# Selective scan and expert routing on one core: the reciprocal of the routing denominator moved between the next unit's two scans, the third chunk's step size computed one and two units sooner, and the second chunk's row scatters moved to units 4 to 11 of the last chunk

## The chip, the cores and the metric

One core of one Trainium2 chip runs the whole program in one launch. The metric is the time of one execution on the device, in microseconds (us); lower is better. The engines are TensorE (PE, with its weight loads shown as PEld), VectorE (DVE), ScalarE (ACT), GpSimd (POOL) and SyncE (SP, which only issues transfers). Each engine runs its own instructions strictly in the order in which the program wrote them; semaphores order them between engines.

## What is computed

The input is x of shape (2, 1024, 128), which is 2048 tokens. Two sublayers follow, each with a residual and a layer norm. Cut to what matters here:

```python
x_in, z = split(x @ W_in); x_conv = silu(conv(x_in) + conv_b)        # 256 channels
Bm, Cm = split(x_conv @ W_x); dt = softplus(x_conv @ W_dt + b_dt)
h = exp(dt * A) * h + (dt * x_conv) * B_t                            # 16 states a channel
y = sum over the states of h * C_t, + x_conv * D, then * silu(z), @ W_out
x = layernorm(x + y)
logits = x @ w_g; the two best of 8 experts; probs = softmax over {top two, -1e9 elsewhere}
rank of each token in its expert (cumulative count), dropped at capacity 640
out = sum over the two experts of prob * (gelu(x @ c_fc[e]) @ c_proj[e])
x = layernorm(x + out)
```

## The kernel before, in words

**Chunks and units.** The tokens are worked on in four chunks of 512 (q = 0 to 3; "third chunk" is q = 2, "last chunk" q = 3), each chunk in 16 units, one for each state n of the scan. So there are 64 units, U = 16 q + n, and every engine has one loop `for U in range(LAST + 1)` over them. All times of the main loop below are told by unit. A unit consists of:

- ACT makes the decay exp(dt * A) of the unit (`decays`, L1074).
- PE spreads row n of B over the partitions (`spread_b`, L648) and DVE multiplies dt * u by it (`drives`, L1649), which gives the drive for two channel halves at once. `drive_beside(U)` says which unit's drive DVE makes between the two scans of unit U. For the 14 units in `TURNED` (4, 7, 10, 14, 19, 22, 26, 29, 43, 46, 51, 54, 57, 60) ACT and PE make the drive instead, so DVE has none beside that unit.
- DVE runs the recurrence as two scans of 512 steps, one for each half of the channels (`scan(U, 0)`, then `scan(U, 1)`, L1678).
- POOL multiplies both halves of the state by C (`multiply`, L1436). It waits for both scans.
- PE adds the product into the accumulator y in PSUM (`add_to_y`, L673 and L678).

Three states (`RING`) and four products (`PRODUCTS`) are kept: `scan(U, 0)` waits for the product of unit U - 3, and `multiply(U)` for the sum of unit U - 4.

**What stands between the units.** While the scan of chunk q runs, the output projection and the routing of chunk q - 1 are put between its units, at places written out by hand in tables indexed by q: `SORT`, `MARK`, `RANK`, `SCORE`, `EXPS`, `ADD`, `SHARE`, `PLACE`. The part that the change touches is the softmax weight of the two chosen experts, which goes back and forth between POOL and DVE:

- `score(q - 1)` on POOL at n = `SCORE[q]` (10, 11, 9 for q = 1, 2, 3), behind that unit's multiply: nine small operations. It ends with `above`, of which ACT takes the exponentials.
- `add_exps(q - 1)` on POOL one unit later (n = `ADD[q]`), behind that unit's multiply: three small operations that end with the denominator (L1497).
- `share(q - 1)` on DVE at n = `SHARE[q]` (12, 13, 11; units 28, 45 and 59): it waits for the denominator and takes its reciprocal (L1766, `share_ready`).
- `weigh(q - 1)` on POOL at n = `SHARE[q]`, behind that unit's multiply: it waits for `share_ready` and gives the two weights (L1501, `weight_ready`).
- `place_weights(q - 1)` on DVE at n = `PLACE[q]` = `SHARE[q]` + 1 (units 29, 46, 60, all of them in `TURNED`), after the unit's second scan: it waits for `weight_ready` and writes the weights into the rows to be sent (L1808).

**The scatters.** Each chunk has 8 indirect transfers (`scatter`, L1517) that POOL issues, four with the first choice and four with the second choice of 128 tokens each, into `slot_rows`. They stand behind a unit's multiply. Chunk 0's stand in units 29 to 36; chunk 1's in units 46, 47 and 48 to 53; chunk 2's in units 60 and 61 and then behind the loop, where the last chunk's 8 follow. A first-choice scatter of chunk q also waits until the second-choice scatters of the chunks before have landed.

**dt of the next chunk.** ACT computes softplus in steps (`take_dt_job`, `soften_exp`, `soften_log`), POOL adds its two parts (`finish_dt`, L1454) and multiplies by u (`times_u`, L1466), each of 128x1024 values, long before chunk q + 1 needs them. In chunk 1 these stand at n = 6 (`soften_log`, L1139), 7 (`finish_dt`) and 9 (`times_u`).

**The end of the loop.** The last unit's product is shared: POOL takes half 0, DVE half 1 (L1835). PE adds the products of units 62 and 63 (L673, L690), DVE gates the result (L1690), PE projects it, and sort, ranks and weights of the last chunk follow on DVE. Only then do the last chunk's scatters go out, and the experts can start when those have landed.

Of the kernel before, what the change touches and what calls it, by code (L numbers as in the profile page):

```python
# [21 lines left out]
NQ = TOKENS // CH  # L22
# [64 lines left out]
def layer_program(nc, x, W_in, channel_values, conv_rows, W_x, W_dt, A_log, W_out, w_g, c_fc, c_proj, out):  # L87
    with ExitStack() as ctx:
# [891 lines left out]
        def _(act):  # L980
# [252 lines left out]
            for U in range(LAST + 1):  # L1233
# [30 lines left out]
                if q < NQ - 1:  # L1264
                    first = 5 if q == 0 else q
                    if n == first:
                        take_bc(q + 1)
                    elif n == first + 1:
                        take_dt_job(q + 1, 0)
                    elif n == first + 2:  # L1270
                        take_dt_job(q + 1, 1)
                    elif n == first + 3:
                        soften_exp(q + 1)
                    elif n == (first + 4 if q == 0 else first + 5):
                        soften_log(q + 1)
# [99 lines left out]
        def _(gp):  # L1375
# [145 lines left out]
            def scatter_some(q, first, count):  # L1521
                for i in range(first, first + count):
                    scatter(i // TPC, TPC * q + i % TPC)

            EARLY = [D_STATE - n for n in PLACE]
            U_PLACE = (NQ - 1) * D_STATE + PLACE[NQ - 1]
            for U in range(LAST + 1):
                q, n = divmod(U, D_STATE)
                multiply(U)
                if q < NQ - 1:  # L1530
                    if n == (6 if q == 0 else q + 1):
                        split_bc(q + 1)
                    elif n == (10 if q == 0 else 6 + q):
                        finish_dt(q + 1)
                    elif n == (11 if q == 0 else 8 + q):
                        times_u(q + 1)
                if q:
# [6 lines left out]
                    if q == 1 and n == PLACE[q]:  # L1544
                        gp.wait_ge(rows_cleared, 16 * 2 * CLEARS)
                        gp.wait_ge(sent_tagged, 1)
                    if n >= PLACE[q] and U < LAST - 1:
                        scatter_some(q - 1, n - PLACE[q], 1)
                    if q >= 2 and n < RUNS // NQ - EARLY[q - 1]:
                        scatter_some(q - 2, n + EARLY[q - 1], 1)  # L1550
            scatter_some(NQ - 2, LAST - 1 - U_PLACE, RUNS // NQ - (LAST - 1 - U_PLACE))
# [27 lines left out]
        def _(dve):  # L1579
# [231 lines left out]
            for U in range(LAST + 1):  # L1811
                q, n = divmod(U, D_STATE)
                scan(U, 0)
                if drive_beside(U):
                    drives(drive_beside(U))
                scan(U, 1)
                if q:
# [6 lines left out]
                    if n == RANK[q] + 1:  # L1824
                        take_ranks(q - 1)
                        place(q - 1)
                    if n == SHARE[q]:
                        share(q - 1)
                    if n == PLACE[q]:
# [158 lines left out]
```

## Time and profile before

| | us |
|---|---|
| median of 3 runs | 385.12 (383.41 to 385.39) |
| the profiled execution, its own time | 384.32 |
| its span in the trace | 382.58 |
| busy: DVE / POOL / PE / ACT | 282.6 (74%) / 266.2 (70%) / 286.2 (75%) / 211.8 (55%) |
| units 0 to 63, from the first scan to the end of the last | 24.9 to 255.1 |
| expert layers and the last norm | 283 to 382.6 |

The profile is of one execution. Times in the rows are microseconds from the start of the span. In a timeline a row gives the start, the duration, the engine, the line of the kernel, the operation, the tile written <- the tiles read with their shapes, and how many instructions are merged into the row; in square brackets stands how long the engine was idle before it, and which instruction of another engine ended that wait ("issue" where the profile shows nothing that it waited for). Durations of neighbouring instructions overlap slightly, so the distance from one start to the next is what an instruction takes of its engine.

### The profile page before, as it was taken

What the parts mean: (1) busy time and instruction counts of PE and PEld (TensorE: products, weight loads), DVE (VectorE), ACT (ScalarE), POOL (GpSimd) and SP (SyncE); (2) the same over time, 40 slices, a digit from 0 to 9 for tenths busy, and PEclk for the clock granted to TensorE, in tenths of its full rate; (3) what the DMA queues carried; (4) which work ended last, traced back from release to release, by engine and by line L of the source; (5) the groups of instructions that cost most, each with busy time, mean ns of one, the idle gap of its engine ahead of it and who ended that gap; (6) DMA issues with size and microseconds to landing.
All of it is one profiled execution on the core that took longest, in us unless ns stands there. A gap on an engine that the chain in (4) does not pass through costs nothing. (4 is left out here: it accounts for less than half of the span.)

```text
span 382.6 us, 5173 instructions
## 1 busy us (share of the span) xinstructions
PE 286.2 (75%) x1566; PEld 207.6 (54%) x1566; DVE 282.6 (74%) x429; ACT 211.8 (55%) x425; POOL 266.2 (70%) x226
## 2 busy tenths in 40 slices
PE   8797889678866867786545899774289999998700
PEld 6445547456745544675433454332278888887600
DVE  2699889999999899999899889986021333334565
ACT  2858987969675684777737455744003323331305
POOL 4507689978888999999999876985710555556532
PEclk9999999999999868997885999899589999999965
DMA  7061079473354263232123211001152444222873
GB/s 233 6 224 55 2 240 286 135 194 127 89 168 137 82 199 117 69 100 82 55 73 122 74 64 55 3 15 42 43 155 79 118 126 125 82 82 76 240 204 110
DMA packets 35786, 42.90 MB, mean 112 GB/s; under 512 B 3862, under 2 KB 26331, under 8 KB 35760
## 3 DMA queue, kind: packets, MB, share of 16 engines
q1 hardware_dynamic: 32336, 37.38, 31.9%
q0 software_dynamic: 2304, 4.24, 3.4%
q10 hardware_dynamic: 1120, 0.97, 0.8%
q8 instruction: 12, 0.20, 0.2%
q14 instruction: 14, 0.11, 0.1%
HBM read 30.11 MB, written 12.79 MB: 112 GB/s over the span
## 5 line engine op out<-in xcount | busy, mean ns | idle before, releaser
L1436 POOL TENSOR_TENSOR product<-state,c_wide 128x1024 f32<-128x1024 f32 x64 | 149.9, 2347 | 37.1 <-DVE state L1678 27.5
L1074 ACT ACTIVATE psum<-dt,a_neg 128x512 f32<-128x512 f32 x96 | 65.0, 686 | 53.1 <-DVE state L1678 51.8
L678 PE MATMUL psum<-ident,product 128*128 128x128 f32 x384 | 56.1, 295 | 24.5 <-POOL product L1436 24.5
L678 PEld LDWEIGHTS psum<-ident,product 128*128 128x128 f32 x384 | 47.4, 152 | 35.0 <-POOL product L1436 32.1
L1678 DVE TENSOR_TENSOR_SCAN state<-psum,drive 128x512 f32<-128x512 f32 x52 | 62.0, 1212 | 2.5 <-ACT psum L1074 2.3
L1649 DVE TENSOR_TENSOR drive<-dtu,psum 128x1024 f32<-128x1024 f32 x50 | 60.0, 1199 | 4.6 <-PE psum L648 4.5
L1678 DVE TENSOR_TENSOR_SCAN state<-psum,carry,drive 128x512 f32<-128x512 f32 x48 | 60.0, 1269 | 0.2
L1563 POOL DMA_INDIRECT result_rows<-state,result_at x30 | 30.3, 1010 | 40.7 <-DVE state L1892 33.4
L1517 POOL DMA_INDIRECT slot_rows<-sent,scatter_at x32 | 32.9, 1028 | 10.7 <-issue 6.6
L912 PE MATMUL psum<-product,fc_sb 128*128 128x320 f32 x128 | 36.1, 435 | 1.1 <-DVE product L1860 1.1
L1857 DVE TENSOR_SCALAR tags<-c_wide 128x10 f32<-128x10 f32 x8 | 1.3, 164 | 43.4 <-PE psum L901 43.4
L1337 ACT ACTIVATE u<-psum 128x640 f32<-128x640 f32 x16 | 11.3, 704 | 38.6 <-PE psum L912 37.9
L673 PE MATMUL psum<-product,ident 128*128 128x512 f32 x60 | 29.4, 619 | 1.6 <-POOL product L1436 1.6
L912 PEld LDWEIGHTS psum<-product,fc_sb 128*128 128x128 f32 x128 | 22.8, 190 | 11.3 <-issue 2.7
L1337 ACT ACTIVATE z_tok<-psum 128x640 f32<-128x640 f32 x16 | 11.3, 704 | 27.6 <-PE psum L912 18.8
L664 PE MATMUL psum<-ident,drive_t 128*128 128x128 f32 x112 | 18.7, 296 | 8.6 <-DVE drive L1649 7.6
L723 PE MATMUL psum<-x_chan,w_conv 128*128 128x512 f32 x48 | 23.4, 614 | 1.6 <-ACT sent L1178 1.6
L1105 ACT ACTIVATE drive_t<-dtu_t,b_t 128x256 f32<-128x256 f32 x56 | 23.7, 494 | 1.0 <-PE psum L664 0.9
L664 PEld LDWEIGHTS psum<-ident,drive_t 128*128 128x128 f32 x112 | 14.4, 152 | 16.1 <-issue 14.3
L648 PE MATMUL psum<-bc_parts,selector 128*128 128x512 bf16 x50 | 20.0, 404 | 2.0 <-DVE state L1678 1.5
L1678 DVE TENSOR_TENSOR_SCAN state<-decay_sb,carry,psum 128x512 f32<-128x512 f32 x16 | 19.6, 1261 | 0.4 <-issue 0.4
L673 PEld LDWEIGHTS psum<-product,ident 128*128 128x128 f32 x60 | 11.5, 200 | 14.0 <-issue 10.7
(256 smaller groups left out, 527.1 us busy)
## 6 DMA issues: line engine op xcount, KB each, us to landing
c_wide<-c_rows SPq DMA_DIRECT2D x32, 512.0 KB
slot_rows<-blank SPq DMA_DIRECT2D x8, 325.0 KB, 4.6
c_wide<-slot_rows SPq DMA_DIRECT2D x8, 325.0 KB, 3.4
result_rows<-zeros SPq DMA_DIRECT2D x8, 256.0 KB, 5.1
late_rows<-zeros SPq DMA_DIRECT2D x8, 256.0 KB
fc_sb<-in_c_fc SPq DMA_DIRECT2D x8, 256.0 KB
proj_sb<-in_c_proj SPq DMA_DIRECT2D x8, 256.0 KB
c_wide<-result_rows SPq DMA_DIRECT2D x8, 256.0 KB, 5.5
```

What stands on the lines that cost most here:

```text
L664: last = nc.tensor.transpose(psum[:, turned_bank(U, d), j * P:(j + 1) * P], drive_t[:, j, d * P:(d + 1) * P], ident[:, :])
L673: nc.tensor.matmul(psum[:, Y_BANK + d, :], ident[:, :], product[:, i, d, :], start=False, stop=True, skip_group_check=True).then_inc(summe ...
L678: last = nc.tensor.matmul(y_part(j, d), product[:, i, d, j * P:(j + 1) * P], ident[:, :], is_transpose=True, start=False, stop=True, skip_ ...
L723: last = nc.tensor.matmul(psum[:, bank, :], w_conv[:, k, d * P:(d + 1) * P], x_of(q, k), start=(k == 0), stop=(k == D_CONV - 1))
L912: last = nc.tensor.matmul(psum[:, 2 + 2 * (h % 2) + s, 0:HALF], fc_sb[:, i, h * P:(h + 1) * P], rows_chan[:, i, s * HALF:(s + 1) * HALF], ...
L1074: nc.scalar.activation(psum[:, A_BANK + d, :], dt[:, q % 2, d, :], ACT.Exp, scale=a_neg[:, n:n + 1]).then_inc(decay_ready, 1)
L1105: nc.scalar.activation(drive_t[:, j, :], dtu_t[:, j, :], ACT.Copy, scale=b_t[:, q % 2, j, n:n + 1]).then_inc(drive_t_ready, 1)
L1436: nc.gpsimd.tensor_tensor(product[:, U % PRODUCTS, channels, :], state[:, U % RING, channels, :], wide, ALU.mult).then_inc(product_ready, 1)
L1517: gp.indirect_dma_start(out=slot_rows, out_offset=bass.IndirectOffsetOnAxis(ap=scatter_at[:, k, j:j + 1], axis=0), in_=sent[:, k, j, :], i ...
L1563: gp.indirect_dma_start(out=result_rows, out_offset=bass.IndirectOffsetOnAxis(ap=result_at[:, i, s:s + 1], axis=0), in_=rows_out[:, i, s, ...
L1649: nc.vector.tensor_tensor(drive[:, drive_number(U) % 2, :, :], dtu[:, q % 2, :, :], psum[:, b_bank(U), :].unsqueeze(1).to_broadcast([P, DT ...
L1678: nc.vector.tensor_tensor_scan(state[:, U % RING, d, :], decay, rows, before, ALU.mult, ALU.add).then_inc(scanned, 1)
```

## The change

Four edits:

- `share(q - 1)` on DVE moves from behind the second scan of unit `SHARE[q]` (28, 45, 59) to between the two scans of the unit after it (29, 46, 60), which are units without a drive on DVE.
- In chunk 1, `soften_log(2)` on ACT moves from n = 6 to n = 5.
- In chunk 1, `finish_dt(2)` on POOL moves from n = 7 to n = 6, and `times_u(2)` from n = 9 to n = 7. The other chunks' stay where they were.
- Chunk 1's 8 scatters move from units 46 to 53 to units 52 to 59 (n = 4 to 11 of the last chunk). Chunk 0's, chunk 2's and chunk 3's stay.

```diff
@@ ACT's loop
                     elif n == first + 3:
                         soften_exp(q + 1)
-                    elif n == (first + 4 if q == 0 else first + 5):
+                    elif n == first + (5 if q == 2 else 4):
                         soften_log(q + 1)
@@ POOL's loop
-            EARLY = [D_STATE - n for n in PLACE]
+            EARLY = D_STATE - PLACE[1]
...
-                    elif n == (10 if q == 0 else 6 + q):
+                    elif n == (10, 6, 8)[q]:
                         finish_dt(q + 1)
-                    elif n == (11 if q == 0 else 8 + q):
+                    elif n == (11, 7, 10)[q]:
                         times_u(q + 1)
...
-                    if n >= PLACE[q] and U < LAST - 1:
+                    if n >= PLACE[q] and q != 2 and U < LAST - 1:
                         scatter_some(q - 1, n - PLACE[q], 1)
-                    if q >= 2 and n < RUNS // NQ - EARLY[q - 1]:
-                        scatter_some(q - 2, n + EARLY[q - 1], 1)
+                    if q == 2 and n < RUNS // NQ - EARLY:
+                        scatter_some(0, n + EARLY, 1)
+
+                    if q == 3 and PLACE[q] - RUNS // NQ <= n < PLACE[q]:
+                        scatter_some(1, n - PLACE[q] + RUNS // NQ, 1)
@@ DVE's loop
                 scan(U, 0)
                 if drive_beside(U):
                     drives(drive_beside(U))
+                if q and n == SHARE[q] + 1:
+                    share(q - 1)
                 scan(U, 1)
...
-                    if n == SHARE[q]:
-                        share(q - 1)
                     if n == PLACE[q]:
                         place_weights(q - 1)
```

## Rows read from the trace of the kernel before

**Rows 1.** Last chunk: length; PE, PEld, DVE, ACT, POOL busy; PE's clock, DMA share, GB/s
```profile
196.90:255.10 58.20, 45.18 (x154) 24.15 (x152) 55.33 (x71) 36.42 (x72) 49.52 (x39) 0.85 0.17 57
```

**Rows 2.** Groups by line: the scatters and the logarithm of dt
```profile
L1517 POOL DMA_INDIRECT slot_rows<-sent,scatter_at x32 | 32.9, 1028 | 10.7 <-issue 6.6 <-DVE sent L1808 3.9 <-PE psum L678 0.2
...
L1139 ACT ACTIVATE soft<-soft 128x1024 f32<-128x1024 f32 x3 | 3.1, 1046 | 0.0
```

**Rows 3.** Timeline of DVE in chunk 1, units 27 to 29
```profile
118.88 1.26 DVE L1678 TENSOR_TENSOR_SCAN state<-psum,carry,drive 128x512 f32<-128x512 f32 x1
...
128.26 0.18 DVE L1766 RECIPROCAL denom<-denom 128x4 f32<-128x4 f32 x1 [1.23 <-POOL denom L1497]
...
130.81 0.14 DVE L1808 TENSOR_TENSOR sent<-weight,psum 128x8 f32<-128x8 f32 x1
```

**Rows 4.** Timeline of POOL in chunk 1, units 25 to 28 (times_u, then three multiplies)
```profile
117.93 2.35 POOL L1466 TENSOR_TENSOR dtu<-dt,u 128x1024 f32<-128x1024 f32 x1
120.25 2.34 POOL L1436 TENSOR_TENSOR product<-state,c_wide 128x1024 f32<-128x1024 f32 x1
...
125.14 2.36 POOL L1436 TENSOR_TENSOR product<-state,c_wide 128x1024 f32<-128x1024 f32 x1
...
128.18 2.36 POOL L1436 TENSOR_TENSOR product<-state,c_wide 128x1024 f32<-128x1024 f32 x1
```

**Rows 5.** Timeline of POOL in chunk 2, units 42 to 45
```profile
178.20 2.35 POOL L1436 TENSOR_TENSOR product<-state,c_wide 128x1024 f32<-128x1024 f32 x1 [0.93 <-issue]
...
190.61 0.20 POOL L1497 TENSOR_TENSOR denom<-denom,others 128x4 f32<-128x4 f32 x1
190.76 2.35 POOL L1436 TENSOR_TENSOR product<-state,c_wide 128x1024 f32<-128x1024 f32 x1
193.07 0.21 POOL L1501 TENSOR_TENSOR weight<-exps,denom 128x8 f32<-128x8 f32 x1
```

**Rows 6.** Timeline of DVE in chunk 2, units 45 and 46
```profile
190.84 0.18 DVE L1766 RECIPROCAL denom<-denom 128x4 f32<-128x4 f32 x1 [1.58 <-POOL denom L1497]
...
193.31 0.17 DVE L1808 TENSOR_TENSOR sent<-weight,psum 128x8 f32<-128x8 f32 x1
```

**Rows 7.** Timeline of POOL in the last chunk, the multiplies of units 55 to 62
```profile
226.47 2.37 POOL L1436 TENSOR_TENSOR product<-state,c_wide 128x1024 f32<-128x1024 f32 x1 [1.20 <-PE psum L673]
231.16 2.37 POOL L1436 TENSOR_TENSOR product<-state,c_wide 128x1024 f32<-128x1024 f32 x1 [2.32 <-DVE state L1678]
234.64 2.36 POOL L1436 TENSOR_TENSOR product<-state,c_wide 128x1024 f32<-128x1024 f32 x1 [1.11 <-issue]
...
239.54 2.35 POOL L1436 TENSOR_TENSOR product<-state,c_wide 128x1024 f32<-128x1024 f32 x1
...
242.72 2.35 POOL L1436 TENSOR_TENSOR product<-state,c_wide 128x1024 f32<-128x1024 f32 x1
...
245.41 2.36 POOL L1436 TENSOR_TENSOR product<-state,c_wide 128x1024 f32<-128x1024 f32 x1 [0.19 <-issue]
...
249.37 2.34 POOL L1436 TENSOR_TENSOR product<-state,c_wide 128x1024 f32<-128x1024 f32 x1 [0.36 <-issue]
...
252.93 3.57 POOL L1436 TENSOR_TENSOR product<-state,c_wide 128x1024 f32<-128x1024 f32 x2
```

**Rows 8.** Timeline of DVE: unit 60's weights, and behind the last scan
```profile
245.26 0.17 DVE L1808 TENSOR_TENSOR sent<-weight,psum 128x8 f32<-128x8 f32 x1
...
255.15 1.91 DVE L1835 TENSOR_TENSOR product<-state,c_wide 128x512 f32<-128x512 f32 x1
259.05 0.69 DVE L1690 TENSOR_TENSOR z_last<-z_last,psum 128x512 f32<-128x512 f32 x1 [1.99 <-PE psum L690]
```

**Rows 9.** Timeline of PE: the sum of unit 62
```profile
256.21 1.88 PE L673 MATMUL psum<-product,ident 128*128 128x512 f32 x4
```

**Rows 10.** Busy time by stretch, columns as in Rows 1, where PE's clock falls
```profile
120.00:122.00 2.00, 0.00 (x0) 0.00 (x0) 2.00 (x3) 0.69 (x1) 2.00 (x2) 1.00 0.81 236
...
124.00:126.00 2.00, 2.00 (x8) 1.30 (x7) 2.00 (x3) 1.59 (x6) 1.67 (x6) 0.50 0.01 4
```
## The prediction

> **What bounds the kernel now.** I read the busy time by stretch first, then the timelines of DVE and POOL side by side around each place that the diff touches, then PE's behind the last scan. The stretch of the last chunk shows DVE busy 55.3 us of 58.2, POOL 49.5 and PE 45.2 [rows 1]: DVE is the engine that carries the loop, and the time of the loop is DVE's work plus DVE's waits. Two of those waits are the ones that the change goes for. In chunk 1 DVE stands 1.23 us before its reciprocal [rows 3], in chunk 2 1.58 us [rows 6], both times until POOL's last operation on the denominator. In the last chunk no wait is shown there. But POOL comes close behind: a multiply takes 2.32 us from start to start (193.07 - 190.76 is 2.31, 120.25 - 117.93 for `times_u` 2.32) [rows 4, 5], a unit 58.2 / 16 = 3.6, and everything else that POOL does has to fit between. A scatter is 1.03 us of POOL by itself [rows 2]; from one multiply to the next with a scatter between they are 252.93 - 249.37 = 3.56 us apart [rows 7], so a scatter costs POOL 3.56 - 2.32 = 1.24 us. Idle time of POOL is what pays for moved scatters, and the question of each part is whether POOL is early or late where it lands.
>
> **Part 1, chunk 1: dt sooner and the reciprocal.** Today `times_u` sits between the multiplies of units 25 and 26 [rows 4], so unit 26's starts at 120.25, though its scans end where the next scan starts plus the small overlap, about 118.95 [rows 3]. With `times_u` and `finish_dt` moved two and one units up, POOL is free at 117.93 and takes unit 26 right behind its scans, at about 119.07. The rest is POOL's own sequence: from unit 26 to 27 4.89 us with the score between, from 27 to 28 3.04 with the sum of the exponentials [rows 4]. So unit 27 starts at 123.96 and unit 28 could at 127.00. The denominator is ready now at 128.26, 3.12 us after unit 27's start; it will be at about 127.08. DVE came to the reciprocal at 128.26 - 1.23 = 127.03. So this move alone takes nearly all of the wait away; the move of the reciprocal behind scan(29, 0) gives another 1.2 us of room. What is late next is the weights. POOL multiplies unit 28 from about 127.16 on, `weigh` ends 2.52 us later (193.28 - 190.76) at 129.68 [rows 5]. DVE needs 0.18 + 2.37 us for reciprocal and two scans (130.81 - 128.26 - 0.18) and is at `place_weights` at 129.58, so it waits some 0.1 us and writes at about 129.71 where it wrote at 130.81 [rows 3]: 1.1 us gained. The cost: the two moved operations of 2.36 us meet POOL in units 22 and 23, where they put product 23 and 24 about 1.2 us later; POOL has caught up by unit 25, and the ring allows two units. On ACT the logarithm of 1.05 us [rows 2] now runs before the two copies of y in unit 21, not after; PE takes them and then spreads B for a drive. Bounds for that are 0 and 1.05; I take 0.1, near the lower end, because the delay has to pass through PE, which works ahead of DVE, before it meets DVE. Part 1 comes to -1.0 us, with bounds -1.23 (the whole wait) and -0.1.
>
> **Part 2, chunk 2: the reciprocal.** Nothing ahead of it on POOL is moved here. DVE is at the reciprocal 1.58 us before 190.84, at 189.26; two scans take 193.31 - 190.84 - 0.18 = 2.29 us [rows 6]. After the change it makes scan(46, 0) first, until 190.40, and waits 0.44 for the denominator, which still ends at 190.81 [rows 5]. Then reciprocal and scan(46, 1), until about 192.17, and there stands `place_weights`, which waits for `weigh`. `weigh` is behind the multiply of unit 45, which starts at 190.76 in any case, and ends at 193.28; `place_weights` starts at 193.31 today. So it will start at 193.31 again: of the 1.58 us, 0.44 stay at the reciprocal and 1.14 turn up before the weights. POOL is what is late, since unit 42's multiply at 178.20, the last before which it was idle, with `times_u`, score, the sum and `weigh` between. Part 2 is worth 0; bounds -1.14 (if the weights did not hold DVE) and 0.
>
> **Part 3: the scatters.** They leave units 46 to 51, where no scan or drive of DVE's waited for a product, so nothing is gained there. Two of the eight stay in units 52 and 53. Six are new in units 54 to 59, 7.4 us of POOL's time. Idle time of POOL that can take them [rows 7]: 1.20 before unit 55, 2.32 before 56, 1.11 before 57. So the scatters of units 54 and 55 cost nothing, and the one of 56 delays unit 57 by 0.1. From there POOL has no room. Unit 58's multiply goes from 239.54 to 234.72 + 4.90 + 1.24 = 240.86 (4.90 is the distance in the rows, the score between). Unit 59's: 240.86 + 3.04 + 1.24 = 245.14, where it is 242.72 now (3.04 as in chunk 1, where no wait lies between). `weigh` ends 2.52 us behind at 247.66. DVE comes to `place_weights` of unit 60 at about 245.2 and today does it at 245.26 [rows 8]; it will wait until 247.68. That is +2.4 us on DVE, and a wait in the place of the one that the change removes. The denominator itself, ready at 240.86 + 3.12 = 243.98, meets DVE between the scans at about 243.7, and its 0.3 are part of those. Then unit 60's multiply starts at 247.6 + 1.24 = 248.85 (now 245.41), and with 3.56 us each unit 61's at 252.4 (249.37) and unit 62's at 256.0 (252.93), 3.1 us later. The last scan ends 2.4 us later less about 0.2 of small waits that are then covered, at 257.3, where 255.15 is the start of what follows it now [rows 8].
>
> The end: PE adds the product of unit 62 at 256.21 now [rows 9], 1.0 us after it was ready at 252.93 + 2.32 = 255.25: PE comes to it behind work that waits for the last scan. It will be ready at 258.3, and PE free for it at 258.4, so the sum comes 2.2 us later; DVE's half product, gating, sort and the last scatters follow at the same distances. New too: the second-choice scatter in unit 59 stands ahead of the first-choice one in unit 60 that waits for its landing, with a multiply of 2.3 us between. I take that as enough; if it is not, a wait of up to one more such length would come on top. The six scatters behind the loop end before the last weights are there, with 3.9 us to spare now (POOL's wait for L1808) [rows 2], and 3.9 - 3.1 + 2.2 = 3.0 then. Part 3 comes to +2.2; bounds 0 and +3.1, and +5.4 with a slow landing.
>
> DVE's half product behind the last scan takes 1.91 us where an operation of the same shape takes 0.69 [rows 8]; it starts beside POOL's multiply. The Trainium skill (SBUF — State Buffer, "Who interferes with whom") has a DVE instruction with two SBUF inputs contend with a GpSimd one that reads SBUF, and the later one wait fully; the row agrees. By that rule the half product could wait for POOL's later end, near 260 at worst, about when PE would come to it anyway, so the sum would stay.
>
> **The sum.** -1.0 + 0 + 2.2 = +1.2 us. The profiled execution took 384.32 (span 382.58) and would take 385.5. The median of the runs is 385.12, 0.8 above it; I give the forecast on the median: 386.3, which is 0.3% up. About 0.5%, 1.9 us, is what a measurement of this kernel can tell from no change.
>
> **Rivals.** *POOL has the room.* If the scatters did not delay the weights of unit 60 (because POOL's idle time of 1.20 + 2.32 + 1.11 + 0.19 = 4.8 us in units 55 to 60 [rows 7] was usable as a whole, or units 46 to 51 gave some back) and DVE gained in chunk 2, the sum would be -1.0 - 1.14 = -2.1 us: 383.0. For it speaks that both waits are plain in the rows; against it that `weigh` ended 0.03 us before DVE used it in chunk 2 and that the last POOL idle time before unit 58 is 1.11 us. It decides by whether unit 59's multiply starts before 243. Chance 0.09. *Parts cancel or none does anything*, with the wait at the weights of unit 60 near 1 us: 384 to 385.5. Chance 0.2.
>
> *The clock of PE at the end (slower).* PE's granted clock fell to 0.5 (1.2 GHz) in chunk 1 behind a stretch without work: none in the one from 120, half clock in the one from 124 [rows 10]. In the last chunk it averages 0.85 [rows 1]. With products 59 to 62 up to 3.1 us later, PE does the same work behind unit 58 in a longer time. A sum takes it 1.88 us [rows 9], and a product comes every 3.56. If that drops the clock, the matmuls behind the last scan, of which unit 62's sum is 1.88 us and unit 63's the same again with the projection as much once more, run at half speed for half or all of 5.6 us: +2.8 to +5.6, 3 in the middle of what is likely, so 386.3 + 3 = 389.3. It decides by the granted clock behind 255; the gaps that I count, 3.56 - 1.88 = 1.7 us, are shorter than the empty stretch in chunk 1. Chance 0.14, with the slow landing in it. The Trainium skill (TensorE: Matmul & The Clock Gate, "Why this matters for your kernels") has the clock go down when PE is idle between bursts. By that rule the rows agree.
>
> **The numbers.** Forecast 0.57, the rivals 0.09, 0.2 and 0.14. The range takes the first rival in and goes up to the clock's: 383.0 to 389.3. Slower by over 0.5% (above 387.05): the clock's 0.14, and a fifth of the forecast's case, where part 3 costs its upper bound: 0.26 together. Faster by over 0.5% (below 383.2): 0.09. Within: 0.65.
>
> **What would show it.** Right: no wait before the reciprocal of unit 29; a wait of about 0.4 before the one of unit 46 and one of about 1.1 before its weights; about 2.3 us of DVE's waiting before the weights of unit 60, ended by POOL's L1501; unit 59's multiply above 2 us behind its scan; units 52 to 62 on POOL without idle time from 57 on. Wrong: a unit 60 without a wait, or a chunk 2 that is shorter by 1 us, or PE's half clock behind 255.

## The result and the profile after

The changed kernel takes 389.53 us (median of 6 runs, 387.6 to 390.42), the kernel before 385.19 in the same runs (383.41 to 385.44): ratio 1.0121, 95% interval 1.0094 to 1.0148. It is 1.2% slower. The forecast was 386.3, 0.3% slower; the result lies 0.2 us outside its range. The profiled execution took 390.21 us, its span is 388.5.

The medians lie 4.3 us (1.1%) apart, the two profiled executions 5.9: the one of the kernel before is 0.9 us under its median, the one of the changed kernel 0.7 above. The stretches below are those of these two executions. The starts of the scans divide the 5.9 us. "Chunk 1" runs from the first scan of unit 16 to that of unit 32, "chunk 2" to that of unit 48, "last chunk" to the end of the last scan.

| us | to unit 16 | chunk 1 | chunk 2 | last chunk | behind it |
|---|---|---|---|---|---|
| before | 79.51 | 58.38 | 58.97 | 58.19 | 127.5 |
| after | 79.80 | 59.42 | 60.23 | 61.75 | 127.3 |
| forecast | | -1.0 | 0 | +2.2 | 0 |
| measured | +0.3 | +1.0 | +1.3 | +3.6 | -0.2 |

The last chunk has DVE's work unchanged (55.29 us, 55.33 in [rows 1]) in a stretch that is 3.6 us longer, and so has POOL (49.38 and 49.52). The added time is waiting. (The forecast has 2.4 us of waiting in the last chunk, less 0.2 that it covers, and an end that moves with it.) The busy time of that stretch, columns as in [rows 1]:

```profile
199.44:261.19 61.75, 44.93 (x154) 23.37 (x152) 55.29 (x71) 36.42 (x72) 49.38 (x39) 0.89 0.16 54
```

The timeline of DVE answers to [rows 3], [rows 6] and [rows 8]: reciprocal and weights of each chunk (L1769 and L1811 are L1766 and L1808 of before), then what follows the last scan.

```profile
128.83 0.15 DVE L1769 RECIPROCAL denom<-denom 128x4 f32<-128x4 f32 x1
130.29 1.28 DVE L1681 TENSOR_TENSOR_SCAN state<-decay_sb,carry,psum 128x512 f32<-128x512 f32 x1 [1.31 <-issue]
131.49 0.14 DVE L1811 TENSOR_TENSOR sent<-weight,psum 128x8 f32<-128x8 f32 x1
...
133.21 1.22 DVE L1652 TENSOR_TENSOR drive<-dtu,psum 128x1024 f32<-128x1024 f32 x1 [0.39 <-PE psum L648]
...
193.42 0.18 DVE L1769 RECIPROCAL denom<-denom 128x4 f32<-128x4 f32 x1 [0.45 <-POOL denom L1497]
...
195.88 0.17 DVE L1811 TENSOR_TENSOR sent<-weight,psum 128x8 f32<-128x8 f32 x1 [1.07 <-POOL weight L1501]
...
247.43 0.18 DVE L1769 RECIPROCAL denom<-denom 128x4 f32<-128x4 f32 x1 [0.43 <-POOL denom L1497]
...
251.60 0.17 DVE L1811 TENSOR_TENSOR sent<-weight,psum 128x8 f32<-128x8 f32 x1 [2.70 <-POOL weight L1501]
...
261.28 2.86 DVE L1838 TENSOR_TENSOR product<-state,c_wide 128x512 f32<-128x512 f32 x1
265.43 0.69 DVE L1693 TENSOR_TENSOR z_last<-z_last,psum 128x512 f32<-128x512 f32 x1 [1.29 <-PE psum L690]
```

No wait is left before the reciprocal of unit 29. The 1.58 us of unit 46 have become 0.45 and 1.07. Unit 60 waits 0.43 + 2.70 us, both times for POOL. Not in the forecast: 1.31 us between the two scans of unit 29.

The timeline of POOL, answering to [rows 7]: the multiplies of units 57 to 60 and the scatters between them.

```profile
237.96 2.37 POOL L1436 TENSOR_TENSOR product<-state,c_wide 128x1024 f32<-128x1024 f32 x1
...
243.21 1.09 POOL L1517 DMA_INDIRECT slot_rows<-sent,scatter_at  x1 [0.32 <-issue]
244.33 2.36 POOL L1436 TENSOR_TENSOR product<-state,c_wide 128x1024 f32<-128x1024 f32 x1
...
247.20 0.20 POOL L1497 TENSOR_TENSOR denom<-denom,others 128x4 f32<-128x4 f32 x1
247.99 1.04 POOL L1517 DMA_INDIRECT slot_rows<-sent,scatter_at  x1 [0.59 <-PE psum L673]
249.06 2.35 POOL L1436 TENSOR_TENSOR product<-state,c_wide 128x1024 f32<-128x1024 f32 x1
251.36 0.20 POOL L1501 TENSOR_TENSOR weight<-exps,denom 128x8 f32<-128x8 f32 x1
251.73 1.03 POOL L1517 DMA_INDIRECT slot_rows<-sent,scatter_at  x1 [0.16 <-issue]
252.78 2.37 POOL L1436 TENSOR_TENSOR product<-state,c_wide 128x1024 f32<-128x1024 f32 x1
```

And PE ahead of unit 29, first before, then after. Before, the sum of a product (L678) waited 3.14 us for POOL, and the convolution (L723) followed with no idle time ahead of it:

```profile
122.64 1.58 PE L678 MATMUL psum<-ident,product 128*128 128x128 f32 x8 [3.14 <-POOL product L1436]
...
124.87 2.77 PE L723 MATMUL psum<-x_chan,w_conv 128*128 128x512 f32 x4
127.48 0.60 PE L664 MATMUL psum<-ident,drive_t 128*128 128x128 f32 x4
```
```profile
122.19 1.09 PE L678 MATMUL psum<-ident,product 128*128 128x128 f32 x8 [1.98 <-POOL product L1436]
...
125.56 3.78 PE L723 MATMUL psum<-x_chan,w_conv 128*128 128x512 f32 x4 [1.83 <-ACT u L1143]
129.14 1.06 PE L664 MATMUL psum<-ident,drive_t 128*128 128x128 f32 x4
```

The turned drive that the second scan of unit 29 reads (L664, 129.14) stands behind a convolution that starts 0.7 us later and runs at half clock. DVE's "<-issue" wait ends 130.29, when that drive is there. In both kernels the convolution starts right behind ACT's copy of its first half out of the bank (L1143), first before, then after:

```profile
124.14 0.67 ACT L1143 ACTIVATE u<-psum,channel_sb 128x512 f32<-128x512 f32 x1
```
```profile
124.84 0.67 ACT L1143 ACTIVATE u<-psum,channel_sb 128x512 f32<-128x512 f32 x1
```

### The profile page after: what moved, and what is told of

It reads as the page before. It is cut to its first block and busy times, and to the rows that moved or that the text cites. A ratio compares the mean times of both kernels' runs of the same rounds, so it can differ in the third digit from the quotient of the medians.

```text
span 388.5 us, 5173 instructions
## 1 busy us (share of the span) xinstructions
PE 288.8 (74%) x1566; PEld 207.3 (53%) x1566; DVE 284.1 (73%) x429; ACT 211.8 (55%) x425; POOL 265.8 (68%) x226
## 5 line engine op out<-in xcount | busy, mean ns | idle before, releaser
L678 PE MATMUL psum<-ident,product 128*128 128x128 f32 x384 | 55.6, 293 | 22.4 <-POOL product L1436 22.2
L1652 DVE TENSOR_TENSOR drive<-dtu,psum 128x1024 f32<-128x1024 f32 x50 | 60.1, 1202 | 6.4 <-PE psum L648 6.4
L678 PEld LDWEIGHTS psum<-ident,product 128*128 128x128 f32 x384 | 47.1, 151 | 32.7 <-POOL product L1436 29.3
L673 PE MATMUL psum<-product,ident 128*128 128x512 f32 x60 | 28.5, 603 | 6.4 <-POOL product L1436 6.4
L723 PE MATMUL psum<-x_chan,w_conv 128*128 128x512 f32 x48 | 24.4, 637 | 2.7 <-ACT u L1143 1.8
L664 PE MATMUL psum<-ident,drive_t 128*128 128x128 f32 x112 | 19.2, 302 | 7.2 <-DVE drive L1652 6.2
L664 PEld LDWEIGHTS psum<-ident,drive_t 128*128 128x128 f32 x112 | 14.8, 156 | 15.5 <-issue 13.7
```

What stands on the lines that cost most here:

```text
L664: last = nc.tensor.transpose(psum[:, turned_bank(U, d), j * P:(j + 1) * P], drive_t[:, j, d * P:(d + 1) * P], ident[:, :])
L673: nc.tensor.matmul(psum[:, Y_BANK + d, :], ident[:, :], product[:, i, d, :], start=False, stop=True, skip_group_check=True).then_inc(summe ...
L678: last = nc.tensor.matmul(y_part(j, d), product[:, i, d, j * P:(j + 1) * P], ident[:, :], is_transpose=True, start=False, stop=True, skip_ ...
L723: last = nc.tensor.matmul(psum[:, bank, :], w_conv[:, k, d * P:(d + 1) * P], x_of(q, k), start=(k == 0), stop=(k == D_CONV - 1))
L1652: nc.vector.tensor_tensor(drive[:, drive_number(U) % 2, :, :], dtu[:, q % 2, :, :], psum[:, b_bank(U), :].unsqueeze(1).to_broadcast([P, DT ...
```

## The experiments

All ratios are to the kernel before, run beside it on the same chip.

**Each part alone.** e1 moves only the reciprocal:

```diff
                 scan(U, 0)
                 ...
+                if q and n == SHARE[q] + 1:
+                    share(q - 1)
                 scan(U, 1)
...
-                    if n == SHARE[q]:
-                        share(q - 1)
```

> Before with only the reciprocal moved between the next unit's scans. Theory 1 (POOL is late; the reciprocal is not what DVE needs): each wait turns up again at the weights one scan later. Chunk 1: the reciprocal of unit 29 waits under 0.1 us, the weights wait until about 130.7, as before, gain 0.1 us; chunk 2: 0.44 us at the reciprocal and 1.1 at the weights of unit 46, gain 0; chunk 3: nothing. Sum 385.1 within 0.5. Theory 2 (the move itself costs, since a reciprocal between two scans breaks them up): the whole difference of the changed kernel, some 2 us or more, is here already: 387 or above. Theory 3 (the move frees DVE as it reads): 382.4.

Measured: 385.98 us, 1.0009 (0.999 to 1.0028), as the first theory has it. The profile shows waits moved from the reciprocals to the weights, 1.23 to 1.00 and 1.58 to 0.45 + 1.06:

```profile
127.80 0.18 DVE L1766 RECIPROCAL denom<-denom 128x4 f32<-128x4 f32 x1
127.98 1.28 DVE L1678 TENSOR_TENSOR_SCAN state<-decay_sb,carry,psum 128x512 f32<-128x512 f32 x1
130.26 0.17 DVE L1808 TENSOR_TENSOR sent<-weight,psum 128x8 f32<-128x8 f32 x1 [1.00 <-POOL weight L1501]
```

e2 has only `soften_log`, `finish_dt` and `times_u` sooner:

```diff
-                    elif n == (first + 4 if q == 0 else first + 5):
+                    elif n == first + (5 if q == 2 else 4):
...
-                    elif n == (10 if q == 0 else 6 + q):
+                    elif n == (10, 6, 8)[q]:
...
-                    elif n == (11 if q == 0 else 8 + q):
+                    elif n == (11, 7, 10)[q]:
```

> Before with only the third chunk's dt sooner. Theory 1: POOL has the denominator of chunk 1 ready at about 127.1, so the 1.23 us wait in unit 28 goes, but PE makes the first half of the fourth chunk's convolution at its half clock and turns unit 29's second drive only behind it: DVE waits 1.0 to 1.3 us before the second scan of unit 29, and 0.3 before the drive of unit 23 (the copies of y behind the logarithm). Sum +0.3 to +1.5 us, 385.5 to 386.7. Theory 2 (this part is clean, as forecast): 384.0 to 384.3, no wait in unit 29.

Measured: 385.85 us, 1.0009 (0.9991 to 1.0027). The 1.23 us are gone, but units 23, 29 and 30 wait 0.30 + 0.96 + 0.22 and chunk 1 is 59.21 us, 0.8 longer; chunk 2 is 60.14, 1.2 longer, with 1.5 us of waits in units 40 and 41. The profile of e2 has both extra lengths of the changed kernel. It is of an execution 1.3 us above e2's median; by the medians this part costs 0.09% (-0.09 to +0.27%).

e3 has only the scatters (the last hunks of POOL's loop):

> Before with only the second chunk's scatters in units 52 to 59. Theory 1: POOL is full from unit 56 on; unit 59's multiply starts 3 us or more behind its scan, the denominator is about 2 us late for the reciprocal behind unit 59's scans and the weights of unit 60 wait another 1 to 1.5. Units 59 to 61 take 3.2 to 3.6 us more, the run 388.4 to 389.0. Theory 2 (the clock of PE at the tail and in chunk 3 is what costs): unit 60 as before, chunk 3 long by its units 48 to 54 and by the sums behind the last scan.

Measured: 387.94 us, 1.0079 (1.0053 to 1.0105). Chunk 1 is as before (58.40), chunk 2 0.4 us longer (59.34), the last is 60.89, 2.7 longer:

```profile
244.18 0.18 DVE L1769 RECIPROCAL denom<-denom 128x4 f32<-128x4 f32 x1 [1.62 <-POOL denom L1497]
...
248.35 0.17 DVE L1811 TENSOR_TENSOR sent<-weight,psum 128x8 f32<-128x8 f32 x1 [1.54 <-POOL weight L1501]
```

The wait at unit 60 is POOL's and the scatters' alone. e4 is the changed kernel without them (e1's and e2's edits):

> The changed kernel with the scatters where they were before. Theory 1: no wait at the weights of unit 60; what is left is the convolution at half clock in units 29 and 30: 385.5 to 387. If the three parts just add up, this is e1 + e2 - before, and the changed kernel is this + e3 - before. Theory 2 (parts fight): above 388 although the scatters are back.

Measured: 386.07 us, 1.0017 (0.9997 to 1.0036); chunks 59.26, 60.14 and 58.62, unit 60 waits 0.27. 0.17% here (0.7 us) and 0.79% in e3 (3.0 us) are 0.96% of the 1.21%; the rest is within the intervals. The profile of e4, too, is of an execution above its median, by 1.3 us.

**The same scatters two units sooner**, on e4 (`q == 3 and 2 <= n < 10`, units 50 to 57):

> The changed kernel with the second chunk's scatters in units 50 to 57, two units sooner. Theory 1 (POOL's idle time ends at unit 57): only the scatter of unit 57 is too many. It puts unit 58's multiply 1.2 to 1.5 us later and unit 59's 1.3 us behind its scan; the weights of unit 60 wait 1.0 to 1.5 us where the changed kernel's wait 2.7 and e4's 0.3. The run is 1 us above e4's, 387. Theory 2 (the scatters cost by themselves, wherever they stand in the last chunk): as the changed kernel, 389.5. Theory 3 (any place before the weights is free): as e4, 386.1.

Measured: unit 60 waits 0.48 + 1.00 us. The last chunk is 59.92, 1.3 longer than in e4: in the profile the first theory's wait is there. The median, 388.39 us (1.0098, 1.0071 to 1.0126), is 2.3 above e4 and not the 1 expected; the profiled span is only 0.9 above, since e4's profiled execution is 1.3 us above e4's median and e5's is at its own. By its median e5 lies between the first theory (387) and the second (389.5) and can't be told from the changed kernel (1.0094 to 1.0148).

**What holds chunk 1.** In e6, on e4, one of the two taps of the convolution in unit 28 goes to unit 29 (1 + 3 in the place of 2 + 2):

```diff
-                        conv_job(3, 1, range(2 * (n - 12), 2 * (n - 11)))
+                        conv_job(3, 1, range(n - 12, (1, D_CONV)[n - 12]))
```

> e4 (reciprocal and dt as in the change, scatters as before) with the convolution of the fourth chunk's second half split 1 + 3 taps over units 28 and 29 in place of 2 + 2, so that less of it stands ahead of unit 29's second turned drive. Theory 1a (it is only the order on PE): the 1.3 us wait before the second scan of unit 29 is gone, and the run is 1.3 us below e4's. Theory 1b (PE is the bound of units 28 to 30 as long as its clock is at half): the wait moves to unit 30's drive, which stands behind the same matmuls; units 28 to 32 together are as long as in e4, 14.9 us, the run 386.1.

Measured: 385.68 us, 1.0018 (0.9995 to 1.004). Unit 29's wait is gone and the drive of unit 30 waits in its place; PE as a whole is late:

```profile
130.24 0.17 DVE L1808 TENSOR_TENSOR sent<-weight,psum 128x8 f32<-128x8 f32 x1 [0.28 <-POOL weight L1501]
130.41 1.28 DVE L1678 TENSOR_TENSOR_SCAN state<-psum,carry,drive 128x512 f32<-128x512 f32 x1
132.95 1.22 DVE L1649 TENSOR_TENSOR drive<-dtu,psum 128x1024 f32<-128x1024 f32 x1 [1.25 <-PE psum L648]
```

So e8, on e4, gives PE work to do in its idle time: the spread of B for unit 30 is done 9 times, the first turned drive of unit 29 5 times, into the same place.

```diff
+                for _ in range(8 if U == 30 else 0):
+                    nc.tensor.matmul(psum[:, b_bank(U), :], selector[:, n, :], bc_parts[:, q * CH:(q + 1) * CH], start=True, stop=True)
...
+                for _ in range(5 if U == 29 and d == 0 else 1):
```

> e4 with repeated matmuls on PE (unit 30's B row 9 times, unit 29's first turned drive 5 times, both with the same result) where PE stood idle ahead of the fourth chunk's convolution. Theory 1 (the granted clock is the cause in chunk 1): the clock stays at 1.0 from 118 to 130, a half of the convolution takes 1.9 us and not 3.8, the wait before unit 29's second scan falls from 1.3 to at most 0.4 and unit 30's goes; the run is 1 to 1.7 us below e4's, 384.4 to 385.1, unless a later stretch loses the clock in its place. Theory 2 (order, or ACT's copy alone): the wait stays above 1 us, 386.1.

Measured: 385.03 us, 0.9997 (0.9975 to 1.0018), 1.0 us under e4 by the medians, with intervals that overlap. In the profiles the work added to PE took 1.5 us out of chunk 1 (57.78 us, 59.26 in e4). The busy time by stretch, of the changed kernel and then of e8 (PE's clock is the third number from the end):

```profile
120.00:130.00 10.00, 6.19 (x22) 3.56 (x22) 8.87 (x13) 6.12 (x12) 8.96 (x15) 0.68 0.63 168
```
```profile
120.00:130.00 10.00, 10.00 (x59) 6.81 (x58) 9.60 (x16) 6.21 (x13) 9.00 (x17) 1.00 0.57 189
```

e5 shows the same without any added work. Up to unit 49 it is the changed kernel, but in its profiled execution the half clock came at 112.0 to 118.9, and from 120 to 130 the granted clock was 1.00. The same convolution then takes 1.99 us behind an even longer wait for ACT, and unit 29 has no wait before its second scan:

```profile
126.25 1.99 PE L723 MATMUL psum<-x_chan,w_conv 128*128 128x512 f32 x4 [2.47 <-ACT u L1143]
128.07 0.60 PE L664 MATMUL psum<-ident,drive_t 128*128 128x128 f32 x4
```

Unit 27, which is near the earlier half clock, waits 1.04 us for PE instead.

**The weights sooner, in the place of the change.** e7 is the kernel before with the sum of the exponentials right behind the score, and `weigh` ahead of the multiply:

```diff
+                if q and n == SHARE[q]:
+                    weigh(q - 1)
                 multiply(U)
...
                         score(q - 1)
-                    if n == ADD[q]:
-                        add_exps(q - 1)
-                    if n == SHARE[q]:
-                        weigh(q - 1)
+                        add_exps(q - 1)
```

> The kernel before, with the small operations on POOL taken ahead of the multiplies that they stood behind: the sum of the exponentials right behind the score, weigh ahead of unit SHARE's multiply. Reciprocal, dt and scatters as before. Theory 1 (what DVE waits for in chunks 1 and 2 is a multiply that POOL makes first): both waits, 1.23 and 1.58 us, go and none turns up at the weights; the last scan ends 2 to 2.8 us sooner, the run is 382.5 to 383.5. Theory 2 (POOL's total work is the bound, the order does not matter): the waits turn up elsewhere, at the ring or the drives; 385.2.

Measured: 384.3 us, 0.9979 (0.9955 to 1.0003), above the 382.5 to 383.5 of the first theory and no gain that is clear of noise. Both waits of [rows 3] and [rows 6] are gone, but PE is late next: unit 30 waits 1.02 us, unit 47 1.80.

```profile
189.03 0.15 DVE L1765 RECIPROCAL denom<-denom 128x4 f32<-128x4 f32 x1
...
191.32 0.14 DVE L1807 TENSOR_TENSOR sent<-weight,psum 128x8 f32<-128x8 f32 x1
...
194.42 1.22 DVE L1648 TENSOR_TENSOR drive<-dtu,psum 128x1024 f32<-128x1024 f32 x1 [1.80 <-PE psum L648]
```

**Keeping PE busy everywhere: a miss first.** e9 (on e8), e10 (on e7, with e8's repeats) and e11 (on the changed kernel, with them) put transposes of the identity into the bank of PE's next job, ahead of the sum of a product (20 in unit 38, 12 in unit 39; e10 and e11 also in units 45 to 50).

> The kernel with parts 1 and 2 and with PE kept busy ahead of chunk 1's end, and now also repeated transposes of the identity on PE in its idle stretches of units 38 (20 of them) and 39 (12); their results are overwritten. Theory (PE's low clock makes the waits of units 40 and 41): the granted clock stays at 1.0 from 158 to 172, DVE's 0.64 in unit 40 and 0.65 + 0.24 in unit 41 shrink to 0.5 in sum or less, the loop is 1.0 shorter, about 384.0 us. Rival (the order of PE's work alone makes them late, whatever the clock): the three waits stay at about 1.5 in sum and the time at 385.0.

> The version that I expect to be the fastest: the kernel before with the weights sooner (sum of the exponentials right behind the score, weights ahead of the multiply), and with PE kept busy by repeated work in its idle stretches (spread of B 9 times for unit 30, the turned drive of unit 29 5 times, transposes of the identity in units 38, 39, 45, 46, 48 and 50). Theory (with both reciprocal waits gone what is left is PE at half clock): the waits of 1.02 in unit 30, 0.74 in units 39 and 40, 1.80 in unit 47 and 1.00 in unit 52 lose 2.5 of their 4.6 us, about 382 us, under both kernels. Rival (the waits come from POOL's products or from the order on PE): 384.3 as with the weights sooner alone.

> The changed kernel itself, with PE kept busy by the same repeated work. Theory (the 1.2 us by which chunk 1 and the 1.2 us by which chunk 2 are longer than before come from PE's clock, and the scatters hold DVE 3.4 us at unit 60 whatever the clock): 1.31 in unit 29, 0.39 in unit 30 and 1.6 in units 40 and 41 shrink to 1.0 in sum; the 0.43 + 2.70 of unit 60 stay; about 387.2 us against 389.5, which leaves about +2 to the kernel before. Rival (the clock is no part of it): 389.5.

Measured: 387.05 (1.0065, 1.0045 to 1.0085), 391.93 (1.0193, 1.0167 to 1.0218) and 395.14 us (1.0293, 1.0261 to 1.0325). The added work waits for the bank, which ACT empties late, and all of PE's queue behind it waits too, the spread of B for the drive of unit 40 with it (e9, timelines of PE, then of DVE):

```profile
160.58 3.43 PE L709 MATMUL psum<-ident 128*128 128x128 f32 x20 [2.92 <-ACT y_chan L1181]
163.81 1.72 PE L681 MATMUL psum<-ident,product 128*128 128x128 f32 x8
```
```profile
165.78 1.22 DVE L1661 TENSOR_TENSOR drive<-dtu,psum 128x1024 f32<-128x1024 f32 x1 [3.05 <-remote]
```

In e10 and e11 DVE waits another 5.12 and 6.25 us in unit 46. On the clock in chunk 2 these runs decide nothing. In chunk 1 e9 and e11 repeat e8, e11 on the changed kernel itself (57.78 and 57.79 us; 59.42 without the repeats). And they say that what fills an idle stretch must not wait for anything itself.

**With work that is ready.** e12 (on e4), e13 (on e7), e14 (on the changed kernel) and e15 (on the kernel before) all have the same edit: repeats of spreads and turned drives whose bank and inputs are free.

```diff
+            SPREADS = {30: 9, 50: 10}
+            TURNS = {(29, 0): 5, (43, 0): 5, (46, 0): 3, (46, 1): 4, (51, 0): 5, (51, 1): 3}
+            AHEAD = {32: 10, 38: 12, 39: 6}
...
+                if U in AHEAD:
+                    spread_b(drive_beside(U + 1), AHEAD[U])
                 if q and n < 2:
                     add_to_y(U - 2)
```

> Parts 1 and 2 with PE kept busy in chunk 1 as in the run before, and by repeated work that is ready in its idle stretches of chunk 2 and 3: the next spread of B 10, 12 and 6 times ahead of the sum of a product in units 32, 38 and 39, the spread of unit 50 10 times, and turned drives 3 to 5 times in units 43, 46 and 51. Theory (clock): the granted clock stays at 1.0 from 134 to 172 and from 200 to 213, the waits of units 40 and 41 (1.53 in sum) fall to 0.9 or less (0.76 + 0.24 was what the delayed run kept at full clock), the 1.79 of unit 52 to 1.0 or less, about 383.7 us against 385.0. Rival (order of the work): both waits stay, 385.0.

> The kernel before with the weights sooner, and the same repeated work. Theory (clock): 4.6 us of waits in units 30, 39, 40, 47 and 52 fall to 2.5 or less, about 382.5 us, under the kernel before by 0.6%. Rival: the wait of 1.80 in unit 47 is for PE's order (a turned drive and a spread behind a product that POOL finishes late) and stays, 384.

> The changed kernel with the same repeated work. Theory (1.03 + 1.25 us of chunks 1 and 2 and 0.7 at unit 52 are the clock, 3.4 at unit 60 are POOL's): about 387.0 us, the waits of unit 60 unchanged at 0.43 + 2.70. Rival (the clock has no part beyond chunk 1): 388.3.

> The kernel before with the same repeated work on PE as e12. Theory (parts 1 and 2 are worth the forecast 1 us where PE's clock is held): 384.5 us, 1.0 above e12, with the waits of 1.23 and 1.58 before the reciprocals in units 29 and 46 still there and those of units 40, 41 and 52 small. Rival (the waits of parts 1 and 2 are replaced by others with the clock held too): 383.5, as e12.

| | us (median) | ratio, 95% interval | chunk 1 | chunk 2 | last chunk | behind it |
|---|---|---|---|---|---|---|
| e15: before | 384.01 | 0.9973 (0.995 to 0.9997) | 58.41 | 58.81 | 56.90 | 128.1 |
| e12: parts 1 and 2 | 383.46 | 0.9954 (0.9932 to 0.9976) | 57.80 | 58.82 | 56.92 | 127.7 |
| e14: the changed kernel | 387.24 | 1.0047 (1.0018 to 1.0077) | 57.80 | 59.00 | 59.86 | 130.0 |
| e13: weights sooner | 383.06 | 0.995 (0.9926 to 0.9973) | 58.21 | 57.14 | 56.24 | 130.1 |

In the changed kernel the repeated work takes 2.3 us off (387.24 against 389.53): 4.7 in the loop of the profiled executions, of which 2.7 are lost again behind it. Of the waits over 0.4 us that e15 does not have, POOL's are left, those of unit 46 (0.42 + 1.07, in the place of e15's 1.58) and those of unit 60 (e14):

```profile
242.24 0.18 DVE L1778 RECIPROCAL denom<-denom 128x4 f32<-128x4 f32 x1 [0.49 <-POOL denom L1506]
...
246.40 0.17 DVE L1820 TENSOR_TENSOR sent<-weight,psum 128x8 f32<-128x8 f32 x1 [2.71 <-POOL weight L1510]
```

Busy time by stretch for units 38 to 41 and 48 to 51, columns as in [rows 1], first the changed kernel, then e14:

```profile
160.00:172.00 12.00, 7.35 (x39) 6.40 (x38) 10.88 (x10) 8.12 (x15) 11.41 (x7) 0.72 0.20 62
198.00:213.00 15.00, 8.11 (x36) 6.12 (x36) 15.00 (x14) 9.61 (x20) 9.59 (x5) 0.61 0.24 84
```
```profile
160.00:172.00 12.00, 11.76 (x88) 9.23 (x85) 12.00 (x12) 9.94 (x22) 11.72 (x7) 1.00 0.26 93
198.00:213.00 15.00, 10.55 (x61) 7.22 (x61) 15.00 (x14) 8.55 (x17) 10.16 (x5) 1.00 0.23 71
```

DVE has no wait in units 40, 41 and 52 of e14, where it had 0.62, 1.00 and 1.83 us. For these units the rival of order is out: the same sequence at full clock is in time. In unit 30 of e7 and e13 it is not the clock: the wait is 1.02 and 1.01 us, with the clock at 1.00 from 126 to 132 in both, and the spread of B stands behind a sum that waits for POOL's product (0.63 and 0.56 us) and a half of the convolution.

**Behind the loop.** In e13 and e14 the stretch behind the last scan took 130 us, in the other kernels so far 126.6 to 129.1. In e13 PE ends its 26 matmuls of the identity 1.23 us before the rows are there, and the first expert's layer takes 6.23 us; e12 has 4.54. First e13, then e12:

```profile
280.00 0.77 PE L910 MATMUL psum<-ident,c_wide 128*128 128x128 f32 x5 [1.23 <-DMA c_wide<-slot_rows]
281.85 6.23 PE L921 MATMUL psum<-product,fc_sb 128*128 128x320 f32 x16 [1.08 <-DVE product L1868]
```
```profile
282.04 0.71 PE L910 MATMUL psum<-ident,c_wide 128*128 128x128 f32 x5
283.83 4.54 PE L921 MATMUL psum<-product,fc_sb 128*128 128x320 f32 x16 [1.08 <-DVE product L1869]
```

e16 is e13 with `range(34)` for `range(26)` there:

> e13 with 34 in the place of 26 matmuls of the identity on PE (about 2 us more at half clock, 1.2 at full) ahead of the turning of the first rows. Theory (in e13 this work ended 1.2 us before the rows were there, PE's granted clock fell at 281.9, and the first expert's layer took 6.23 us where it takes 4.54): no half clock behind 280, the stretch from the last scan to the end 127.5 and not 130.0 us, 381 us in the median. Rival (the 2.5 us come from the loading of the rows or of the weights): 130.0 us, 383 us.

Measured: 383.06 us, 0.9942 (0.992 to 0.9964), the median of e13. The layer is back at 4.54 us, which gives 1.7, but the first rows are turned 29.9 us behind the last scan (29.1 in e13, 28.3 in e12), and the stretch is 130.3 us. The longer fill took 0.7 us of it. Another 1.2 us were lost behind the start of the last expert's layer (31.6 us from there to the end, 30.4 in e13 and 30.5 in e12), by what is not shown. The theory was right on the cause of the slow layer and wrong on the gain.

## Why the prediction was wrong, step by step

In short: the sum's +1.2 us left out that TensorE's clock could fall where DVE follows PE closely inside the loop, took the earlier logarithm as nearly free, and priced the scatters 0.7 us too low. By the ratios the scatters alone cost 3.0 us (e3; forecast +2.2), parts 1 and 2 together 0.7 (e4, -0.1 to +1.4; forecast -1.0), and the whole change 4.7 (3.6 to 5.7; forecast +1.2).

**Part 2 was right.** 0.44 and 1.14 us were forecast, 0.45 and 1.07 came; e12 and e15 have 58.82 and 58.81 us for chunk 2. The reciprocal and the weights hang on one queue of POOL's, and moving DVE's reader moves only the wait.

**Part 1 was right on POOL and wrong on ACT and PE.** The step that failed is the cost of the earlier logarithm: "because the delay has to pass through PE, which works ahead of DVE", taken as 0.1 out of 0 to 1.05. With the clock held the part gives 57.80 - 58.41 = -0.6 (e12 and e15): the wait of 1.27 us before the reciprocal goes and 0.28 come back before the weights, which is the forecast's -1.0, but the drive of unit 23 waits 0.30 us for PE, behind copies of y that ACT makes 1.2 us later in the chunk (102.08, before 100.64). At the clock that the kernel has, chunk 1 is 0.8 us longer in e2 and 0.9 in e4: 1.32 + 0.23 us of waits in units 29 and 30 of e4, which e8 removes by keeping PE busy. PE was not ahead of DVE. Behind unit 23's wait DVE and ACT are 0.4 us later in the chunk, so the copy that frees the convolution's bank is too; POOL's earlier product lets PE add it 0.45 us sooner. Between the two PE stood idle for another 1.83 us, and at the half clock behind that the next four matmuls took 3.78 us.

**Part 3 was right in mechanism and too small.** POOL has no room from unit 57 on and the weights of unit 60 are late, as forecast; "about 2.3 us" of waiting is 3.1. Counted from the first scan of unit 58, unit 58's multiply was forecast at 6.44 and came at 6.67, unit 59's at 10.72 and came at 11.40. The term is the price of a scatter: 1.24 us between two multiplies, but 0.2 and 0.45 us more where it stands behind the small operations of the score and the sum, since the idle time ahead of it is then 0.32 and 0.59 and not 0.17 (the same in e3, e11 and e14; the cause is not shown). With the clock held the part costs 59.86 - 56.92 = 2.9 us in the loop (e14 and e12), alone 2.7 (e3).

**What no term held: chunk 2 and unit 52.** Chunk 2 is 1.3 us longer in the changed kernel and 1.2 in e2 and e4, and unit 52 waits 1.83 us, not 1.17. Both are PE at half clock: 0.72 in the mean from 160 to 172, where the kernel before has 1.00. In the last chunk the kernel before has its half clock too, from 198.2 to 211.8; the changed kernel's, from 202.1 to 215.7, is 1.4 us later counted from the start of the chunk, and the matmuls ahead of unit 52's spread (L625) take 3.29 and not 2.64 us. The prediction looked for the clock only behind the last scan. There it was 1.0 from 246 to 272 and that rival did not come about. Its point of decision was wrong: what mattered was where PE falls idle while DVE is close behind it.

The sum at held clock is e14 less e15 over the three chunks: 176.66 - 174.12 = +2.5 us (-0.6, +0.2 and +3.0), for a forecast of +1.2 (-1.0, 0 and +2.2). Of the 5.9 us between the two profiled executions the other 3.3 go with the clock: the changed kernel loses 181.40 - 176.66 = 4.7 us to it in the loop, the kernel before 175.54 - 174.12 = 1.4. Between the medians the share is smaller: with the repeats they lie 3.2 us apart (387.24 and 384.01), without them 4.3.

The half product behind the last scan grew from 1.91 to 2.86 us beside POOL's later multiply. It ended at 264.14, and PE came to its sum (L690) at 264.24, straight from the sum of unit 62, so it did not set the end. In both kernels it ends 0.6 us behind POOL's last product (263.59 after, 256.50 before). The Trainium skill (SBUF — State Buffer, "Who interferes with whom") has a DVE instruction with two SBUF inputs contend with a GpSimd one that reads SBUF. This trace agrees: 2.86 us beside 1.91.

**What stays open:** where PE's clock falls, and so how much of the loss is the edit's. The program alone does not set it. e3 is the kernel before up to unit 45, and yet in its profiled execution the clock is at half from 160.4 to 167.2, and chunk 2 is 0.4 us longer; the profile of the kernel before has 1.00 there. First before, then e3:

```profile
160.00:172.00 12.00, 8.14 (x68) 7.54 (x68) 12.00 (x12) 9.86 (x20) 11.74 (x6) 1.00 0.25 79
```
```profile
160.00:172.00 12.00, 9.83 (x62) 8.84 (x63) 11.38 (x11) 9.25 (x20) 11.37 (x6) 0.72 0.26 87
```

e5's chunk 1 is the other case. Idle time alone does not tell it either: ahead of the sum in unit 38 PE is idle for 3.04 or 3.05 us in e2, e4, the changed kernel, e3 and e1, and the clock falls in all but e1. The edit does have a part in it: chunk 2 takes 60.1 to 60.3 us in all six profiles that have the dt sooner and no work added in chunk 2 (e2, e4, e5, e6, e8, the changed kernel), and 58.5 to 59.3 in the four without (the kernel before, e1, e3, e7). That the half clock costs the time is shown by e8, e12 and e14.

## What to carry to other kernels

A wait between two engines is worth removing only down to the next date that hangs on the same queue: look for who else reads from it, as the weights did here. When an edit makes one engine early, look where TensorE falls idle next and whether its granted clock holds, in every stretch where the bound engine follows closely; repeated matmuls into a place that is rewritten anyway, with nothing to wait for, can be worth more than the edit itself (ratio 0.9973 on the kernel before, an interval that just leaves out 1; 1.0047 in the place of 1.0121 on the changed one). Work that waited for a bank was worse than idle time (e9 to e11). And where the clock falls inside a kernel, one profile of each version is one draw: in e2 and e4 the profiled executions were 1.3 us above their medians, more than the effect in question.

The fastest version run has the weights sooner and PE kept busy (e13, e16): 383.06 us, 0.5 to 0.6% under the kernel before and 1.7% under the changed one. It can't be told from parts 1 and 2 with PE kept busy (e12, 383.46).

## What the runs showed that was not expected

- More work on TensorE made chunk 1 shorter: 10.00 of 10 us busy at clock 1.00 in e8, against 6.19 busy at 0.68 in the changed kernel, and chunk 1 1.5 us shorter than in e4.
- Where the half clock falls changes from execution to execution: e5 and the changed kernel are alike up to unit 49, and in their profiled executions it comes in chunk 1 at 112.0 and at 123.6.
- A scatter of 1.03 us takes POOL 0.17 us of idle time ahead behind a multiply, 0.32 behind the score and 0.59 behind the sum of the exponentials, but 0.16 behind the weights, which like them end with an operation of 0.2 us.
- The same 26 matmuls of the identity do or do not hold the clock for the first expert: with a gap of 1.23 us behind them (e13) and 1.37 (e14) the layer took 6.23 and 6.01 us, with 0.60 (the changed kernel) and none (e12) 4.54. In e13 the layer costs 1.7 us by it; the rows came 0.8 us later than in e12 besides.
